# A state-space block on one core: the dt broadcast of four steps as one DMA over 128 partitions

## The reference, cut to what matters

```python
xn = layernorm(x)                                # x is (8, 512, 128): B=8, T=512, D=128
x  = x + attn(xn) + ffn(xn)                      # ffn: three layers with weights of +-1
# inside attn, E = 256 features, N = 64 states:
xc = silu(conv(rmsnorm(xn) @ in_proj_x)); z = rmsnorm(xn) @ in_proj_z
dt = clip(softplus(xc @ dt_W + dt_b), 0.001, 0.1)     # (B, T, E)
Bp = xc @ B_W; Cp = xc @ C_W                          # (B, T, N)
A  = -exp(A_log)                                      # (N,)
for t in range(T):                                    # the scan
    dA = exp(dt[:, t, :, None] * A)                   # (B, E, N)
    h  = dA * h + dt_t * B_t * x_t
    y[t] = einsum('ben,bn->be', h, C_t)
# then y * silu(z), an output projection, a gated feed-forward layer and the residuals
```

## Time and profile before

| what | value |
|---|---|
| median of two runs | 2100.57 us (2097.97 to 2103.18) |
| the profiled execution | 2099.65 us, span in the trace 2097.5 us |
| PE, DVE, ACT, POOL busy | 60%, 49%, 42%, 41% of the span |
| mean granted TensorE clock | 0.674 of full speed |
| DMA queue of the kernel (q1) | 97760 packets, 319.12 MB, 72.6% of 16 engines |

### The profile page before, as it was taken

One profiled execution on the slowest core, in us unless ns is written; L12 is line 12 of the kernel. 1 busy time (PEld: TensorE's weight loads), 2 busy tenths in 40 slices (PEclk: granted clock), 3 DMA queues, 4 the chain that ended last, 5 costly groups with the idle time before them and its releaser, 6 DMA issues. The chain is left out here.

```text
span 2097.5 us, 27406 instructions
## 1 busy us (share of the span) xinstructions
PE 1261.5 (60%) x8012; PEld 501.4 (24%) x8012; DVE 1017.5 (49%) x2237; ACT 875.7 (42%) x964; POOL 849.6 (41%) x1215
## 2 busy tenths in 40 slices
PE   6990246666555565566555665666655566576558
PEld 3560011222211222122211222122211222122224
DVE  4762255555454445455444444455443445455444
ACT  3772244444343434344433433344433434344442
POOL 4541244444343343444333343444343344344342
PEclk9995555666677667676657556676575666666677
DMA  2227588788778687878878687878878787878871
GB/s 88 98 98 163 120 181 174 159 169 173 165 161 164 151 169 159 164 161 159 172 155 162 149 169 149 170 157 161 171 157 164 144 167 164 160 157 160 168 161 34
DMA packets 97938, 321.18 MB, mean 153 GB/s; under 512 B 9056, under 2 KB 22240, under 8 KB 95456
## 3 DMA queue, kind: packets, MB, share of 16 engines
q1 hardware_dynamic: 97760, 319.12, 72.6%
HBM read 303.37 MB, written 15.73 MB: 152 GB/s over the span
## 5 line engine op out<-in xcount | busy, mean ns | idle before, releaser
L863 POOL TENSOR_TENSOR decayed<-decay,state 128x256 f32<-128x256 f32 x1024 | 725.5, 731 | 1127.0 <-DVE state L1163 1081.1
L1099 ACT ACTIVATE decay<-decay,a_col 128x2048 f32<-128x2048 f32 x256 | 514.0, 2008 | 1002.4 <-DMA decay<-dt_stage 983.8
L1152 DVE TENSOR_TENSOR ps<-decay,ps 128x512 f32<-128x512 f32 x512 | 353.4, 690 | 860.6 <-ACT state L1111 762.7
L917 PE MATMUL ps<-moving,b_rows 36*128 36x256 bf16 x1024 | 264.2, 351 | 752.5 <-DVE ps L1152 734.3
L972 PE MATMUL ps<-state,c_cols 128*32 128x256 f32 x4096 | 460.0, 533 | 0.3 <-issue 0.3
L1163 DVE TENSOR_TENSOR state<-decayed,ps 128x256 f32<-128x256 f32 x1024 | 387.6, 415 | 96.8 <-PE ps L972 58.5
L1111 ACT COPY state<-ps 128x512 f32<-128x512 f32 x512 | 281.7, 583 | 112.1 <-issue 58.7
L917 PEld LDWEIGHTS ps<-moving,b_rows 36*128 36x128 bf16 x1024 | 62.7, 101 | 997.2 <-DVE ps L1152 665.4
L924 PE MATMUL ps<-moving,b_rows 36*128 36x256 bf16 x1024 | 265.4, 352 | 33.0 <-DMA b_rows<-b_stage 33.0
L1057 PE MATMUL ps<-h,w 128*128 128x256 f32 x512 | 238.5, 562 | 0.9 <-DVE h L1285 0.8
L1057 PEld LDWEIGHTS ps<-h,w 128*128 128x128 f32 x512 | 105.7, 252 | 144.1 <-issue 140.1
(11 more groups left out here) (115 smaller groups left out, 883.0 us busy)
## 6 DMA issues: line engine op xcount, KB each, us to landing
decay<-dt_stage SPq DMA_DIRECT2D x256, 1024.0 KB, 14.7
moving<-u_stage SPq DMA_DIRECT2D x64, 288.0 KB
b_rows<-b_stage SPq DMA_DIRECT2D x256, 36.0 KB
dt_stage<-dt_tok SPq DMA_DIRECT2D x8, 512.0 KB, 2.6
u_stage<-u_parts SPq DMA_DIRECT2D x8, 512.0 KB, 2.8
b_stage<-b_parts SPq DMA_DIRECT2D x8, 384.0 KB, 2.8
u_stage<-u_parts SPq DMA_DIRECT2D x8, 256.0 KB, 2.0
x_in<-in_L_attn_x_dram SPq DMA_DIRECT2D x32, 64.0 KB
```

Source lines behind the costliest of these rows:

```text
L863: nc.gpsimd.tensor_tensor(decayed[:, p], decay[:, dec_slot(m, k), p, k % TS, :], state[:, (k - 1) % RING, p * E:(p + 1) * E], ALU.mult).th ...
L917: return nc.tensor.matmul(ps[:, acc_bank(m, k), p * E:(p + 1) * E], b_rows[rows(1), cb, p, kk, :], moving[rows(1), cb, kk, :], start=False ...
L1099: nc.scalar.activation(pair, pair, ACT.Exp, scale=a_col[:, 2:3]).then_inc(decay_ready, 1)
L1152: nc.vector.tensor_tensor(ps[:, acc_bank(m, k), :].rearrange("p (q e) -> p q e", q=HQ), decay[:, dec_slot(m, k), HQ:Q, k % TS, :], ps[:, a ...
```

## The change

The staging tensor gets another order, and the load of a chunk becomes one DMA.

```diff
-    dt_stage = nc.dram_tensor("dt_stage", (2, Q, T, E), F32, kind="Internal").ap()
+    dt_stage = nc.dram_tensor("dt_stage", (2, T // TS, Q, TS, E), F32, kind="Internal").ap()
...
-                        sp.dma_start(dt_stage[bb, q].rearrange("(p j) e -> p (j e)", j=NJ),
+                        sp.dma_start(dt_stage[bb, :, q].rearrange("p j e -> p (j e)"),
                                      dt_tok[:, bb].rearrange("p j e -> p (j e)")
                                      ).then_inc(S[f"dt_stored{bb}"], 16)
...
-                    def load_dt(t, slot, waits):
+                    def load_dt(c, slot, waits):
 
                         wait_all(sp, waits)
-                        for bb in range(2):
-                            sp.dma_start(decay[bb * N:(bb + 1) * N, slot].rearrange("n q t e -> n q (t e)"),
-                                         dt_stage[bb, :, bass.ds(t, TS), :].rearrange("q t e -> q (t e)")
-                                         .unsqueeze(0).broadcast_to([N, Q, TS * E])
-                                         ).then_inc(dt_loaded[slot], 16)
+                        sp.dma_start(decay[:, slot].rearrange("n q t e -> n (q t e)"),
+                                     dt_stage[:, bass.ds(c, 1)].rearrange("b c q t e -> b (c q t e)")
+                                     .unsqueeze(1).broadcast_to([2, N, Q * TS * E])
+                                     ).then_inc(dt_loaded[slot], 16)
...
-                            load_dt(t0 + (kc + 2) * TS, (m * BTS + kc + 2) % NDEC,
+                            load_dt(i * BTS + kc + 2, (m * BTS + kc + 2) % NDEC,
                                     [(self_state[1], used)] if waiting else [])
...
-                            act.wait_ge(dt_loaded[slot], dec_loads(m, r, k) * (16 * 2))
+                            act.wait_ge(dt_loaded[slot], dec_loads(m, r, k) * 16)
```

More of the change, by code:

```diff
@@ L57, in mamba_and_binary_mlp_block @@
     CYCLE = 3
-    assert CYCLE * BTS % NDEC == 0 and CYCLE * STEPS % NACC == 0
+    assert TS == NJ and CYCLE * BTS % NDEC == 0 and CYCLE * STEPS % NACC == 0
     TG = STEPS
@@ L781, in _ @@
                     load_b(0, 0, range(B))
-                    load_dt(TS, 1, [])
-                    load_dt(2 * TS, 2, [])
+                    load_dt(1, 1, [])
+                    load_dt(2, 2, [])
                     load_u(TC, 1, [])
```

## The result

The changed kernel takes 5715.53 us (5715.15 to 5715.91, two runs) against 2100.57 us: a ratio of 2.727, 95% interval 2.710 to 2.745. The forecast was 5,815 us in a range of 5,600 to 6,700. The profiled execution has a span of 5713.8 us at a mean granted TensorE clock of 0.555 (0.674 before). Some executions are some per cent slower whatever the kernel; the ratios leave them out, and since the profiled execution of rep64x2 (2181 us) was one of them, no rate is read from it.

What follows compares the result with a forecast made beforehand. The scan was taken to be bound by the arrival of dt, which the change confines to two engines: 180 us before, 5,589 us for 144.2 MB at 25.8 GB/s, 44 after and 2 outside the span make 5,815 us, range 5,600 to 6,700.

Steps and rivals of the forecast that it cites:

- The bound before: In the scan before the change: bound by how fast 2 MB of dt arrive; ACT waits 983.8 us in 122 waits.
- Two engines: At the new dt load: a source beginning with 2 runs on two engines, 1.049 MB for each engine and chunk.
- The rate of one engine: In the dt load: one engine moves 25.8 GB/s, taken from the stores at 166.5 us.
- the 144.2 MB of one engine: Over the scan, each of two engines carries dt 134.2, u 6.3, B 3.1, x and results at most 0.5 MB.
- the 44 us at the end: After the scan: 44 us from the last wait for dt to the end of the span.
- The row of 24.9 GB/s: Three-engine stretch at 236.5 to 241 us: rate set aside because it contains small packets; would give 6,017 us.
- The cover: In the scan: chunk c+2's load is issued with about 39 us of c+1 left, so the engines never run dry.
- B rows and x tokens behind whole chunks: At DVE's x statistics and PE's first product of a step group: stops up to one chunk, costing nothing in the sum.
- SP held at issues: At SP's DMA issues: held longer than the up to 10.8 us of before, with the same cover.
- Rival A: At the dt load: sixteen engines at full speed, the steps become the bound, 1,365 us; chance 0.04.
- Rival B: At the dt load: two engines, but slow, 18.4 GB/s, in all 8,063 us; chance 0.08.
- rival C: At the dt load: sixteen engines, no faster, limited by repeated reading of the same rows, 2,100 us; chance 0.02.

Runs made afterwards that it cites:

- rep64x2: Against the kernel before: new staging, lower half's dt to every partition, as two DMAs of 64 partitions, each with 64 repetitions in front; 2048.61 us, ratio 0.9786.
- rep128: The changed kernel with its one DMA's source beginning with 128 repetitions, all partitions getting the lower half's dt (wrong result); 1469.46 us, 0.7017 of the kernel before.
- lead64: The changed kernel with source [64, 2, 4096] in place of [2, 64, 4096], mixing up the halves' dt; 1472.27 us, 0.702 of the kernel before.
- copies2: The changed kernel with dt staged twice in DRAM, the one DMA's source beginning with 4; 3238.02 us, 1.535 of the kernel before.
- copies8: The changed kernel with dt staged eight times in DRAM, the one DMA's source beginning with 16; 1905.08 us, 0.9091 of the kernel before.
- halves16k: The changed kernel's staging and 16 KB runs, but two DMAs per chunk again, one per 64 partitions; 2052.64 us, 0.982 of the kernel before.
- halves_u: halves16k with u and B rows reordered, the u source beginning with its 12 rows, B still with 3; 1902.40 us, 0.9074 of the kernel before.

## Why the prediction was right, point by point

*The bound before.* Right. With 16 engines at 21 GB/s in place of 13 the same steps need 1,470 us (rep128, lead64); ACT's wait for dt was what the kernel paid.

*Two engines.* Right, and shown. The DMA share is 13.7% with a leading 2, 0.25 with 4, and 0.70 or more with 16, 64 or 128, at times of 5,716, 3,238 and 1,469 to 2,053 us. The traces also list every packet with its start and duration, and counting how many are under way at once shows the number itself. In the change, two of the 16 KB packets of q1 are under way at once for 4,645 us, and three or more for only 54 us. In copies2 four is the most frequent number (1,906 us). In rep128, lead64, copies8 and halves16k it is 16 (367, 367, 536 and 538 us), with 17 or more for 30 to 64 us, where the records of one packet and the next overlap; 13 comes second, the 16 less the three that carry u or B. So the leading dimension, and not the reading of two rows, the 16 KB runs or the staging, is what confined the load. The Trainium skill's rule (DMA: Bandwidth & Descriptors, "Why a DMA increments its semaphore by 16 and not by 1"), the largest number up to 16 that divides the slowest dimension on both sides, gives 2, 4 and 16 here, and 12 for the u load of halves_u. The traces agree with it.

*The rate of one engine.* The term that was off by its size. I took 25.8 GB/s; from the first packets at 180 us to the last wait's end at 5671.9 the 144.2 MB of one engine took 5,492 us, 26.3 GB/s. The 144.2 MB are my estimate, but the dt packets agree with it: 16,384 bytes in 613 ns, in the change as in copies2, are 26.7 GB/s, and the smaller packets beside them are a little slower. The 5,492 us in place of 5,589 are 97 of the 100 us by which the sum was too long; the 44 us at the end were 42, and the rest is rounding. The row of 24.9 GB/s that I set aside for its small packets was indeed too low. That the 25.8 came within 2% is in part luck: they are the rate of stores, the other direction, in a window of 1.5 us with a share of two digits.

*The cover.* Right: no slice of the scan but the last is under 54 GB/s, and between 200 and 5,671 us there is no moment without a packet under way and only 23 us with a single one. I had placed the release one step late, though. The wait on `self_state` counts steps done, so the load of chunk c+2 is released when chunk c-1 is done, not after the first step of chunk c. The two come close together, because ACT's program has the first exponential of chunk c ahead of its copies of the last steps of chunk c-1, so these end only once chunk c has landed. Where SP is free, the issue therefore comes some 4.5 us after the landing (2977.72 and 2982.23 us above), and the slack of about 39 us is as I gave it. Where SP is held at u, B or x issues, the dt issue comes later, up to 38 us after that landing; the first one of this kind (chunk 3) ends 8 us after chunk 2 has landed, and u and B transfers kept the engines at work until then.

*B rows and x tokens behind whole chunks.* Not seen. I expected steps to stop at them up to one chunk. The only wait of PE for B is 47.9 us, once, at the start of the scan, where the kernel before has one of 33.0 us, and none of DVE for x is in the list. It cost nothing in the sum, as forecast, but the stops themselves were wrong.

*SP held at issues.* Right in direction: up to 15.7 us for one dt issue, 30.1 us for one B issue and 37.6 us for one u issue, under the same cover.

*Rival A* had the mechanism of the width right and its condition wrong: a full-width DMA does reach 21 GB/s per busy engine, but only when it is spread over 16 engines, and its source did not allow that here. Its time of 1,365 us was 105 us too short beside rep128, where ACT still waits 285.1 us for dt. The Trainium skill's point (SBUF — State Buffer, "Door 1: The DMA port swizzle") that 64 partitions reach 8 of 16 ports agrees with the pair of rep128 and rep64x2. The pair shows the halving, not the ports. *Rival B* is excluded by the 26.3 GB/s, *rival C* by lead64, which reads the same rows as often and takes 1,472 us.

*Still open:* why eight copies, on 16 engines and 128 partitions, run at 13.9 GB/s per busy engine, while lead64 and rep128 run at 21. A packet takes 1,233 ns in the one and 619 or 620 ns in the others, with 16 under way in all three. The distance between the copies is excluded. Reading 16 rows as against one or two, and which partitions each engine is given, are both possible; a run that reads one row with a leading 16 would tell them apart and was not made.

## What to carry to other kernels

Before merging broadcasts into one DMA, look at the first dimension of its source: a short one (a pair of halves, three copies) confines the whole transfer to as many engines, and the profile shows it as a DMA share of k/16 while everything waits. Put the long dimension, repetition included, in front, and choose the layout of rows so that it can be. No run here did that in one DMA with the dt that the reference asks for: lead64 has the order, but its layout is not that of the state. A leading 16 alone was not enough either, as copies8 shows. Reading the share beside the GB/s tells two kinds of slow transfer apart: a full share at a low rate means that every packet is slow (here with spans of 64 partitions and with the eight copies), a low share at the full rate means too few engines.

## What the runs showed of the hardware that I had not expected

- Width and engine count are separate: 16 engines move 13.1 GB/s each to spans of 64 partitions (halves16k), 21.4 to 128 (rep128), and also only 13.9 to 128 with a leading dimension of 16 (copies8).
- The median 16 KB packet takes 613 ns with two or four engines at work and 619 or 620 with 16 (lead64, rep128), so most packets of 16 engines still go at full rate; the mean rises from 623 (the change) to 746 ns (rep128). With spans of 64 partitions the median is 1,282 ns (halves16k).
- A load on three engines costs time in which the others idle: giving the u load 12 engines in place of three, with the B rows in another order, made the kernel with two DMAs 7.6% faster (ratios 0.9074 and 0.982) without a change in the rate of a busy engine.
- Issuing the two halves from two queues gave 2.7%, with no higher rate per engine.
